# Selected attention: maxima over tiles of 128 queries, the rest of four heads in one tile, keys loaded in groups of four heads

## The reference, cut to what matters

```python
scores = sigmoid(normed @ Wr + br)
k = round(0.15 * l)                               # 154 of 1024
_, idx = top_k(-scores, k)
q, kk, v = (normed @ W + b).reshape(b, l, 12, 16)  # for Wq, Wk, Wv
probs = softmax(q @ kk^T / sqrt(16))
attn_out = (probs @ v) @ Wo + bo
merged = where(attn_mask, attn_out, mix_out)
```

## Time and profile before

| | us |
|---|---|
| median of three runs | 2219.47 (2218.63 to 2223.66) |
| the profiled execution, its own time | 2225.55 |
| its span, first to last instruction | 2223.8 |
| VectorE busy | 1462.9 (66%) |
| ScalarE busy | 983.7 (44%) |
| mean granted TensorE clock | 0.872 of full speed |

### The profile page before, as it was taken

How to read it: one execution, slowest core, us unless ns; L and a number is a source line. 1 busy time by engine, 2 the same in 40 slices (tenths; PEclk the granted TensorE clock), 3 DMA queues, 4 the chain that set the end, 5 groups by cost and what they waited for, 6 DMA issues and landing times.

```text
span 2223.8 us, 27557 instructions
## 1 busy us (share of the span) xinstructions
PE 1771.5 (80%) x9834; PEld 939.0 (42%) x9834; DVE 1462.9 (66%) x3304; ACT 983.7 (44%) x1371; POOL 119.8 (5%) x163
## 2 busy tenths in 40 slices
PE   1686878998999999974566787899899999998635
PEld 1356447563333333353234554756423333334523
DVE  4747874046777777757767668522577777773875
ACT  0321431234666666742532234121456666666143
POOL 4010000000000000004011000000000000000110
PEclk9877895998999999996578779789989999999856
DMA  5011210012110000000000212000310000000000
GB/s 131 0 34 38 53 26 0 1 45 70 25 26 23 22 22 22 8 1 26 3 29 1 57 39 53 1 1 0 103 26 22 22 24 25 24 15 1 0 0 29
DMA packets 57644, 58.48 MB, mean 26 GB/s; under 512 B 27063, under 2 KB 35556, under 8 KB 57510
## 3 DMA queue, kind: packets, MB, share of 16 engines
q1 hardware_dynamic: 55894, 53.57, 9.2%
q0 software_dynamic: 1616, 3.16, 0.6%
HBM read 38.51 MB, written 18.16 MB: 25 GB/s over the span
## 4 chain that ended last, share of the span: by engine, by line
PE 56%; DVE 36%; issue 4%; ACT 3%; SPq 1%; DMA 1%; POOL 0%; DVEq 0%; ACTq 0%
PE PV L826 8%; PE S L779 7%; DVE nmp L1447 6%; PE ST L735 4%; DVE nmp L1386 4%; PE ST L534 4%; PE S L774 3%; PE ST L806 3%; PE MT L833 2%; DVE junk L1435 2%; DVE Er L1474 2%; PE PV L654 2%; DVE st L1274 2%; PE S L746 2%; DVE R L1494 1%
## 5 line engine op out<-in xcount | busy, mean ns | idle before, releaser
L1447 DVE TENSOR_REDUCE nmp<-S 128x1 f32<-128x512 f32 x768 | 501.6, 687 | 138.3 <-PE S L779 133.3
L1109 ACT ACTIVATE Er<-ST 128x1024 f32<-128x1024 f32 x384 | 392.1, 1023 | 225.6 <-PE ST L806 219.0
L779 PE MATMUL S<-KS,QS 96*128 96x512 bf16 x768 | 302.6, 397 | 23.4 <-DVE U L1437 11.0
L806 PE MATMUL ST<-QS,KS 100*128 100x512 bf16 x768 | 234.8, 387 | 3.0 <-ACT QS L1100 3.0
L779 PEld LDWEIGHTS S<-KS,QS 96*128 96x128 bf16 x768 | 74.4, 97 | 323.1 <-DVE nmp L1447 205.0
L826 PE MATMUL PV<-Er,V 128*17 128x512 f32 x1536 | 203.5, 603 | 0.0
L1386 DVE TENSOR_REDUCE nmp<-S 80x1 f32<-80x512 f32 x192 | 120.0, 678 | 25.9 <-PE S L624 24.4
L434 POOL TENSOR_SCALAR tp<-mv 128x8 f32<-128x8 f32 x20 | 5.2, 258 | 1933.1 <-DVE mv L1278 1933.1
L624 PE MATMUL S<-KS,QS 96*80 96x512 bf16 x192 | 79.9, 448 | 34.0 <-DVE nmp L1386 31.4
L1076 ACT ACTIVATE Er<-ST 128x480 f32<-128x480 f32 x144 | 65.3, 528 | 84.7 <-PE ST L641 84.7
L806 PEld LDWEIGHTS ST<-QS,KS 100*128 100x128 bf16 x768 | 72.9, 100 | 53.9 <-issue 10.2
(11 more groups left out here) (366 smaller groups left out, 3181.7 us busy)
## 6 DMA issues: line engine op xcount, KB each, us to landing
KS<-scr_k SPq DMA_DIRECT2D x576, 32.0 KB, 1.8
scr_k<-R SPq DMA_DIRECT2D x16, 576.0 KB, 3.9
QS<-scr_q SPq DMA_DIRECT2D x288, 32.0 KB, 1.8
scr_q<-R SPq DMA_DIRECT2D x8, 576.0 KB, 3.7
out_dram<-HS SPq DMA_DIRECT2D x8, 384.0 KB, 2.8
QS<-scr_q SPq DMA_DIRECT2D x48, 30.0 KB, 1.8
wf<-in_L_ffn_W_dram SPq DMA_DIRECT2D x2, 576.0 KB
scr_q<-small SPq DMA_DIRECT2D x8, 90.0 KB, 1.9
```

The lines of the kernel that those rows point to most:

```text
L779: ins = nc.tensor.matmul(S[n % 2][:, :], QS[0:KP, k, (u // 2) * P:(u // 2 + 1) * P], KS[0:KP, k, (u % 2) * HALF:(u % 2 + 1) * HALF], start ...
L806: ins = nc.tensor.matmul(ST[i % 2][:, (kt % 2) * HALF:(kt % 2 + 1) * HALF], KS[0:KP + 4, k, kt * P:(kt + 1) * P], QS[0:KP + 4, k, half * H ...
L1109: A_(E[:, g, :], ST[i % 2][:, :], ACT.Exp).then_inc(s["exps"], 1)
L1447: v.tensor_reduce(nmp[:, u // 2, u % 2:u % 2 + 1], S[n % 2][:, :], AX.X, ALU.max).then_inc(s["reduced"], 1)
```

## The change

The maxima are made for groups of four heads. The query slots of a head are now numbered 0 to 159 in one run (the selected 154 first), so that a tile of 128 queries holds most of them; the remaining 32 of four heads make one more tile of 128 rows. A group so has 8 units of 128 x 512 and 2 for the rest (four matmuls into four row groups each). `chain`, `maxrow0` and `mcopy0` run once for each group. The keys of even groups lie in `KS`, those of odd groups in `QS`, whose rows 96 and 97 GpSimd fills with ones at the start of each pair; so heads 0 to 7 need no free place, and head m waits for the scores of head m-8. TensorE's order is written anew: each iteration g makes the exponentials of group g and, between them, the maxima of group g+1. The order of SP's work is not changed. The turned sums are read with an offset of 77 instead of 80, so what follows the stage is as before.

```diff
+        GROUP = 4
+        GROUPS = HEADS // GROUP
+        REST = 2 * QP - P
+        MAXIMA0 = 2 * GROUP + 2
+        SUMS0_AT = {2: 0, 5: 1, 7: 2}
+        KG = [KS, QS]
+        KGR = [KR, QR]
...
-                    if m >= KRING:
-                        sp.wait_ge(s["st0"], p * 72 + 3 * (m - KRING + 1))
-                    load_head(KS, o.scr_k0, h, K_PARTS, KR[h % KRING])
+                    if m >= 2 * GROUP:
+                        sp.wait_ge(s["st0"], p * 72 + 3 * (m - 2 * GROUP + 1))
+                    g = m // GROUP
+                    load_head(KG[g % 2], o.scr_k0, h, K_PARTS, KGR[g % 2][h % KRING])
...
-            link(g.iota(slot_i, pattern=[[QC, 2], [1, QP]], base=0, channel_multiplier=0))
+            link(g.iota(slot_i, pattern=[[QP, 2], [1, QP]], base=0, channel_multiplier=0))
...
+                if p:
+                    g.wait_ge(s["stile"], p * NSTEP)
+                    for o in slots:
+                        g.wait_ge(o.s["hrms"], p * 2)
+                g.memset(QS[KP:KP + 2, :, :], 1.0).then_inc(s["qones"], 1)
+                g.wait_ge(s["qones"], p + 1)
...
+                def unit0(g, x):
+
+                    if g == GROUPS:
+                        return
+                    o, n = slots[g * GROUP // H], MAXIMA0 * g + x
+                    half = x % 2
+                    keys = KG[g % 2][0:KP, :, half * HALF:(half + 1) * HALF]
+                    if x == 0:
+                        for r in range(GROUP):
+                            pe.wait_ge(s[KGR[g % 2][r]], 96 * (LOADS * p + g // 2 + 1))
+                        if g * GROUP % H == 0:
+                            pe.wait_ge(s["q0r"], p * 384 + (o.x * 192 + 192))
+                    pe.wait_ge(s["reduced0"], p * MAXIMA0 * GROUPS + n + 1)
+                    if x < 2 * GROUP:
+                        ins = nc.tensor.matmul(S[n % 2][:, :], o.QS0[0:KP, (g * GROUP + x // 2) % H, 0:P], keys[:, x // 2, :], start=True, stop=True)
+                    else:
+                        for r in range(GROUP):
+                            ins = nc.tensor.matmul(S[n % 2][r * REST:(r + 1) * REST, :], o.QS0[0:KP, (g * GROUP + r) % H, P:2 * QP], keys[:, r, :], start=True, stop=True)
+                    ins.then_inc(s["units0"], 1)
+
+                def maxrow0(g):
+                    if g == GROUPS:
+                        return
+                    pe.wait_ge(s["rowmax"], base + g + 1)
+                    pe.wait_ge(s["mcopied"], base + g + 1)
+                    for i in range(GROUP + 1):
+                        ins = nc.tensor.transpose(MT[KP:KP + 2, i * P:(i + 1) * P], nms[:, g % 2, i, 0, :], identb[:])
+                    ins.then_inc(s["mturned"], 1)
...
+                maxima0(0, 0, MAXIMA0)
                 maxrow0(0)
+                pe.wait_ge(s["qones"], p + 1)
+                for g in range(GROUPS):
+                    n = 3 * GROUP * g
+                    maxima0(g + 1, 0, 3)
+                    exps0(n)
+                    exps0(n + 1)
+                    maxima0(g + 1, 3, 4)
+                    exps0(n + 2)
+                    exps0(n + 3)
+                    maxima0(g + 1, 4, 5)
+                    if g:
+                        pv0(2 * g - 1)
+                    maxima0(g + 1, 5, 6)
+                    exps0(n + 4)
+                    exps0(n + 5)
+                    maxima0(g + 1, 6, 7)
+                    exps0(n + 6)
+                    exps0(n + 7)
+                    maxima0(g + 1, 7, 8)
+                    exps0(n + 8)
+                    exps0(n + 9)
+                    maxima0(g + 1, 8, 10)
+                    exps0(n + 10)
+                    exps0(n + 11)
+                    pv0(2 * g)
+                    maxrow0(g + 1)
                 pv0(H - 1)
...
+                def mcopy0(g):
+                    act.wait_ge(s["mturned"], base + g + 1)
+                    rows = slots[g * GROUP // H].QS0[KP:KP + 2, g * GROUP % H:g * GROUP % H + GROUP, :]
+                    A_(rows[:, :, 0:P], MT[KP:KP + 2, 0:GROUP * P].rearrange("p (h n) -> p h n", h=GROUP), ACT.Copy)
+                    A_(rows[:, :, P:2 * QP], MT[KP:KP + 2, GROUP * P:(GROUP + 1) * P].rearrange("p (h n) -> p h n", h=GROUP), ACT.Copy).then_inc(s["mcopied"], 1)
...
+                for g in range(GROUPS):
+                    for x in range(MAXIMA0):
+                        n = MAXIMA0 * g + x
+                        ve.wait_ge(s["units0"], p * MAXIMA0 * GROUPS + n + 1)
+                        v.tensor_reduce(nmp[:, x // 2, x % 2:x % 2 + 1], S[n % 2][:, :], AX.X, ALU.max).then_inc(s["reduced0"], 1)
+                        if g == GROUPS - 1 and x in SUMS0_AT:
+                            divide(a, SUMS0_AT[x])
```

More of the change, by code:

```diff
@@ L612, in selected @@
             def selected(p):
-                base = p * 48
-                def units0(h, us):
-                    o = slots[h // H]
[L617 to L643, removed]
+                base = p * ROWS
@@ new lines, in maxrow0, with exps0 @@
+                def maxrow0(g):
[6 more added lines that the diff above has]
+                    ins.then_inc(s["mturned"], 1)
+                def exps0(n):
+                    h, i = n // 3, n % 3
+                    g = h // GROUP
+                    o = slots[h // H]
+                    if n % (3 * GROUP) == 0:
+                        pe.wait_ge(s["mcopied"], base + g + 2)
+                    pe.wait_ge(s["ex0"], p * 72 + n + 1)
+                    for kt in range(3 * i, min(3 * i + 3, T)):
+                        ins = nc.tensor.matmul(ring4[n % 4][:, (kt - 3 * i) * 2 * QP:(kt - 3 * i + 1) * 2 * QP], KG[g % 2][0:KP + 2, h % KRING, kt * P:(kt + 1) * P],
+                                               o.QS0[0:KP + 2, h % H, :], start=True, stop=True)
+                    ins.then_inc(s["st0"], 1)
@@ L1069, in selected @@
                 mcopy0(0)
[L1070 to L1080, removed]
+                for n in range(3 * HEADS):
+                    h, i = n // 3, n % 3
+                    w = (3 if i < 2 else 2) * 2 * QP
+                    act.wait_ge(s["st0"], p * 72 + n + 1)
+                    act.wait_ge(s["pv0"], p * HEADS + h + 1)
+                    A_(E0[:, h % RING0, i * 6 * QP:i * 6 * QP + w], ring4[n % 4][:, 0:w], ACT.Exp, scale=float(DH) ** -0.5).then_inc(s["ex0"], 1)
+                    if n % 12 == 11 and n + 1 < 3 * HEADS:
+                        mcopy0(n // 12 + 1)
+                    if n % 18 == 5 and n >= 18:
+                        sums0(n // 18 - 1)
                 sums0(3)
             def attention(p):
-                base = p * 48 + HEADS
+                base = p * ROWS + GROUPS
                 def out_sums(h, part):
@@ L1380, in divide @@
                     ins.then_inc(s["ctxn"], 1)
[L1382 to L1392, removed]
+                for g in range(GROUPS):
[3 more added lines that the diff above has]
+                        v.tensor_reduce(nmp[:, x // 2, x % 2:x % 2 + 1], S[n % 2][:, :], AX.X, ALU.max).then_inc(s["reduced0"], 1)
+                        if g == GROUPS - 1 and x in SUMS0_AT:
+                            divide(a, SUMS0_AT[x])
+                    ve.wait_ge(s["reduced0"], p * MAXIMA0 * GROUPS + MAXIMA0 * g + MAXIMA0 + 2)
+                    if g >= 2:
+                        ve.wait_ge(s["mturned"], base + g - 1)
+                    chain(base, g, P, GROUP + 1, 1)
                 for r in range(3):
```

42 lines of the change are left out of this document (15 added, 27 removed).

## The result

The changed kernel takes 2250.80 us (median of four runs, 2249.14 to 2252.90), the kernel before in runs beside it 2221.56 (four runs, 2218.63 to 2232.31): ratio 1.0125, 95% interval 1.0102 to 1.0147. It is slower, as forecast; the forecast of 2239.7 was 11 us short. The two profiled executions took 2249.14 and 2225.55 us, 23.6 apart, and it is these 23.6 that the rows can explain. The kernel before was profiled in an execution some 4 us above its median, so about 6 us of the difference of medians are in no row.

What follows compares the result with a forecast made beforehand. Bound: key supply, through SP's and TensorE's waits. 238.9 + 4 x 17.0 + 24.5 = 331.4 against 321.3 us, +10.1 a pair; 2219.47 + 20.2 gives 2239.7 us. Own range 2229 to 2252, whole range 2221 to 2261.

Steps and rivals of the forecast that it cites:

- Rival A: Selected attention: VectorE was the bound and keys come in time, so 13 us a pair sooner, 2193 us; chance 0.10.
- the forecast mechanism: Key loads: SP waits on head m-8, TensorE on four heads, leaving about 5 us a group without issue.
- The first wait: Start of the stage: keys for group 1 are in at 238.9 us, after the queries' loads end at 226.43.
- the pitch: SP queue: time from one key DMA's issue to the next, about 0.46 us, from twelve unhindered DMAs in 5.49.
- The period: Time between iteration starts: 17.0 us, near the middle of 15.3 and 19.0, the latter with SP waiting for the second head.
- The tail: Iterations 4 and 5, which wait for no keys: 13 and 9 us, 22 at the high clock; 24.5 taken.
- The hedge for the low clock: End of the stage: at the low clock TensorE binds and iterations 4 and 5 take 33 us, so 24.5 was taken.
- The rest of four heads in one pass: TensorE: four 32-column matmuls into four row groups run side by side, as one pass rather than four of 0.2 us.
- A drain between the modes: TensorE: changing the tiling mode drains the engine, 0.26 us twice per rest block, 0.5 us a group.
- The copies: ScalarE, once per group: two copies of 512 and 128 columns, between 0.6 and 1.3 us together, 0.9 taken.
- POOL: GpSimd's fill of two QS rows with ones: about 3.6 us, costing nothing because the engine stands idle there.
- hand-over: Once per four heads: chain 0.5, transposes 0.6 and copies 0.9 with latencies, about 2.2 us without the next group's exponentials.

Runs made afterwards that it cites:

- e3: The changed kernel, but TensorE waits for one head's keys ahead of that head's first maximum, not for all four of the group; 2190.44 us, ratio 0.9862.
- e1: The changed kernel, but the keys of heads 8 to 23 are never loaded, nor waited for; 2170.94 us, ratio 0.9764 to the kernel before.

## Why the prediction was right, and where not

**Which end bounds the stage: right.** Rival A held that VectorE was the bound and the keys would come in time. For that SP had to issue without a gap, and in the change it did not. e3, which changes only the place of the waits, turns the forecast mechanism off and rival A on: 19.1 us less than the old stage, where rival A had 13. Its last key was in later than rival A had it (287.34 + 1.8, from 227.64: 61.5 us against 57.0), but the rest took 14.2 us from there, not the 24.5 of a full tail, because most of the last maxima had been made while keys still came. That it is the pair of waits, SP on head m-8 and TensorE on four heads, is therefore shown, not argued.

**The first wait.** Forecast: 12.5 us from the end of the queries' loads to group 1. Measured: 223.13 to 237.05, 13.9 (the weight load of that maximum; its matmul follows at 237.08). The step that failed is the pitch, 0.46 us from twelve DMAs; 24 of them took 12.26 us, 0.51 each. The line L340 in two bursts (count, ns to issue one, least, median, most, first and last start), from 240.5 and from 256.5 us, shows where the time goes:

```profile
L340 SPq DMA_DIRECT2D KS<-scr_k x24: 302/420/425, 240.6 to 251.2; - x24
```

```profile
L340 SPq DMA_DIRECT2D QS<-scr_k x24: 302/420/1444, 256.8 to 268.6; - x24
```

The median is the same. In the first of these bursts no DMA takes longer than 0.43 us to issue, in the second, and in the other three of pair 0, the longest takes 1.1 to 1.6. That is nearly all of the difference between 10.96 and 12.2 us, and over all five bursts (59.8 us for 120) it makes 0.50 of 0.46. In pair 1 one burst of five has such a DMA (1.66 us). What stands beside it is in the DMA view of the window 256.5 to 269.5 (packets, MB, share):

```profile
q8 instruction: 1, 0.02, 0.6%
```

In the changed kernel each of the five slow DMAs starts within 0.4 us of one such packet (16 KB each: 79 make 1.29 MB in the whole trace) of the queue that the page lists as q8, instruction; the five bursts without a slow DMA have none. So the slow issue goes with a load of instructions, not with the keys. That it is the cause is likely, but not shown by an experiment. Group 0 was through by 229.0, 5.9 us after the queries' loads, against 5.6 forecast (232 after 226.4).

**The period.** Forecast 17.0 between 15.3 and 19.0. Measured 16.2, 17.5, 17.5, 17.4 us: 17.1 on average, and in pair 1 17.4, 17.0, 17.1, 17.0. Two of the parts are as forecast: 3.6 us until SP may go on (2.7 to 3.7), and 1.6 to 1.8 from the last issue to TensorE's start. The third is right in kind and too large. The prediction let SP wait for the second head, behind a slow L681 block, until 9.2 us into the iteration. The block was slow, as TensorE's timeline of the iteration from 253.26 shows,

```profile
257.49 2.34 PE L681 MATMUL PV<-Er,V 128*17 128x160 f32 x32
```

and SP went on to the second head 7.1 to 7.5 us into each iteration that has such a block early, not at 9.2. Iteration 0 has none, and there SP went on after 6.3 us without a wait. In pair 1 no slow DMA stands in the first head of those iterations, and SP's wait shows (window 1357 to 1361.5):

```profile
SPq L352 <- PE ST L668: 0.9, 1, 0.9
```

In pair 0 the one slow issue fell just there and took most of that time instead; SP waited only 0.3 and 0.4 us more, and not at all in iteration 3. But for the first, 16.2, the periods came out alike, 17.0 to 17.5. So 17.0, chosen "near the middle of 15.3 and 19.0", was right by a choice between two bounds, not by a reckoning of the wait: the wait for the second head adds about 0.9 us to a period, not 2.7. The granted clock by stretch (columns: stretch, length, busy us and count of PE, PEld, DVE, ACT, POOL, then the clock):

```profile
226.00:250.00 24.00, 10.12 (x94) 6.09 (x90) 8.42 (x18) 7.13 (x16) 0.00 (x0) 0.64 0.23 56
250.00:270.00 20.00, 11.04 (x117) 6.22 (x117) 7.07 (x13) 6.74 (x15) 0.00 (x0) 0.67 0.20 50
...
290.00:310.00 20.00, 13.31 (x133) 8.29 (x132) 9.32 (x22) 7.66 (x17) 0.00 (x0) 0.76 0.17 41
310.00:340.00 30.00, 24.05 (x309) 18.06 (x307) 18.00 (x58) 13.46 (x30) 0.00 (x0) 0.98 0.01 2
```

Each iteration that had waited for keys began at 1.2 GHz and ended at 2.4 (the L645 pair 1.01 us at its start, 0.61 in e1 at the high level); with no more idle time, from 310 us on, it is 0.98.

**The tail.** Forecast 24.5, with 22 at the high clock; measured 22.3 (305.62 to 327.90) and 22.4. The hedge for the low clock was not needed: by 310 us the clock had risen. The two parts of the 22 missed in opposite ways: iteration 4 took 14.3 us (305.65 to 319.97) where 13 were forecast, and the rest 7.9 where 9 were. The prediction's own terms for iteration 4 (6.2, three times 1.1, 0.5 and 2.2) add up to 12.2, not 13. Its own range doesn't follow from its terms either: a period of 16.3 with a tail of 23, and 18 with 28, give 2231 to 2255 us, not 2229 to 2252. The first step was 1.4 too short, four periods 0.6, and the tail 2.2 too long. Together 13.9 + 68.6 + 22.3 = 104.8 against a forecast of 105.0: errors of opposite sign. That the sum came out nearer than its terms is luck. Pair 1 was 1.3 us under it.

**The rest of four heads in one pass: right.** TensorE's timeline at the high clock, a full maximum of 128 queries and the four that make one rest tile:

```profile
261.19 0.38 PE L645 MATMUL S<-KS,QS 96*128 96x512 bf16 x1
...
261.88 0.40 PE L648 MATMUL S<-KS,QS 96*32 96x512 bf16 x4
```

Four take as long as one. A drain between the modes, which the prediction priced at 0.5 us a group, can't be told apart from the waits for ScalarE and VectorE that stand in the same places. The copies took 0.59 + 0.25 us together (forecast 0.9).

**POOL: the step that failed.** The memset was costed at "nothing", covered by GpSimd's idle time of 23 us in both pairs. Its length was right (3.51, forecast 3.6) and GpSimd was idle. But the idle time of the engine isn't the whole cover: VectorE, at work beside it, paid 2.5 us in pair 1.

**The sum.** Forecast +20.2, measured 18.6 in the two stages. Beyond them lie 2.5 from the memset, and a net 2.2 in unchanged work: pair 0 reached its selected stage 3.3 us sooner, and the same stretch of pair 1 took 5.3 longer, without the memset's part, of which the 32 matmuls above are 2.7. The forecast had no term for this, and nothing ties the 2.7 to the change. The rest of the distance to the measured median is between runs. So 29 us by the medians where 20 were forecast is not a stage that was mis-sized by 9: the stages came within 1.6 us.

## What to carry to other kernels

A buffer that comes free by heads and is waited for by groups holds back both sides: the producer starts when the consumer has begun, the consumer starts when all of the group has landed, and the period becomes the sum of both. Before widening a ring, put the work's period beside the time that the whole group takes to issue and land; then wait in the unit in which the data are used, and if the queue is then the bound, issue fewer, larger DMAs. An engine that is idle is no free place for an operation until the operations of its neighbour beside it have been looked at.

## What was not expected

- With keys always there the new loop takes 25.5 us a pair less than the old one; rival A, bound by SP's issuing, had 13. The iteration of e1, 8.6 us, is about what the prediction's own terms give (ten maxima 6.2, hand-over 2.2).
- A `TENSOR_SCALAR` of 128x4 took 2.69 us rather than 0.17 beside a memset of two partitions.
- DMAs of 64 KB were issued at the pitch of those of 32 KB (12 in 5.4 us where no wait came between) and landed in 2.2 us rather than 1.8.
- In five of the changed kernel's ten bursts one DMA took 1.1 to 1.7 us to issue, where the median is 0.42, each time beside a 16 KB packet of the instruction queue.
- Unchanged f32 matmuls took 4.1 or 6.8 us with the clock granted where they fell, in kernels whose work up to there is the same.
